# The first batch of three attentions scored in fp32, with the bf16 parts of the other batches made on GpSimd

## The reference, cut to what matters

```python
x = x + tanh(g_xattn[i]) * attention_i(layernorm(x), ctx)
x = x + tanh(g_ffn[i]) * ffn_i(layernorm(x))
```

```python
Q, K, V = heads(x @ Wq + bq), heads(ctx @ Wk + bk), heads(ctx @ Wv + bv)
scores  = Q @ K.T / sqrt(8) + adj          # then masked by mask or by padding
out     = softmax(scores) @ V @ Wo + bo
```

## Time and profile before

| what | value |
|---|---|
| time, median of 3 runs | 862.73 us (861.38 to 862.84) |
| the profiled execution's own time | 862.37 us |
| its span, first to last instruction | 860.4 us |
| mean granted TensorE clock | 0.898 of full speed |
| PE, VectorE, ScalarE, GpSimd busy | 702.3, 573.1, 488.9, 166.6 us |

### The profile page before, as it was taken

One profiled execution on the slowest core, in us unless ns is written; L12 is line 12 of the kernel. 1 busy time (PEld: TensorE's weight loads), 2 busy tenths in 40 slices (PEclk: granted clock), 3 DMA queues, 4 the chain that ended last, 5 costly groups with the idle time before them and its releaser, 6 DMA issues. The chain is left out here.

```text
span 860.4 us, 14382 instructions
## 1 busy us (share of the span) xinstructions
PE 702.3 (82%) x4728; PEld 396.0 (46%) x4728; DVE 573.1 (67%) x1765; ACT 488.9 (57%) x1323; POOL 166.6 (19%) x135
## 2 busy tenths in 40 slices
PE   4589994559997878999744899949999999869978
PEld 2266663336665323333222667635336666644322
DVE  3699995869996358667865999855316666436553
ACT  2288881259883568598812988812666556413201
POOL 8622000420000045536655000020000000000000
PEclk8689997769999768998885999979999999969999
DMA  8895004060000000000009200000000000000000
GB/s 310 169 319 177 2 7 69 23 126 2 2 2 2 0 1 0 1 0 1 1 0 180 41 2 2 2 26 0 1 0 1 1 2 2 1 1 1 0 1 24
DMA packets 22056, 32.26 MB, mean 38 GB/s; under 512 B 1760, under 2 KB 15712, under 8 KB 21216
## 3 DMA queue, kind: packets, MB, share of 16 engines
q1 hardware_dynamic: 21984, 31.36, 14.4%
HBM read 21.39 MB, written 9.96 MB: 36 GB/s over the span
## 5 line engine op out<-in xcount | busy, mean ns | idle before, releaser
L816 ACT ACTIVATE RING<-RING,NMX 128x256 f32<-128x256 f32 x384 | 190.7, 500 | 56.2 <-DVE NMX L1637 55.8
L1637 DVE CUSTOM_DVE_ANT_0 RING<-bank,ADJM 128x256 f32<-128x256 f32 x384 | 143.4, 413 | 23.5 <-DMA scratch<-RING 22.5
L1158 PE MATMUL bank<-W,RING 128*128 128x128 f32 x768 | 120.5, 282 | 15.6 <-ACT RING L828 13.9
L541 POOL TENSOR_TENSOR small<-small 128x8 f32<-128x8 f32 (+2 forms) x13 | 17.7, 1365 | 463.1 <-DVE small L1528 463.1
L1158 PEld LDWEIGHTS bank<-W,RING 128*128 128x128 f32 x768 | 91.7, 145 | 27.9 <-ACT RING L816 23.2
L1138 PE MATMUL bank<-ARENA 128*128 128x256 bf16 x384 | 77.8, 290 | 30.7 <-DMA ARENA<-scratch 25.7
L1649 DVE COPY RING<-bank 128x512 f32<-128x512 f32 x144 | 98.6, 686 | 1.2 <-PE bank L1158 0.8
L816 ACT ACTIVATION_READ_ACCUMULATOR RING<-RING,NMX 128x1 f32 x384 | 72.8, 190 | 0.0
L997 PE MATMUL bank<-XT,W 128*128 128x512 f32 (+2 forms) x118 | 62.2, 668 | 6.6 <-ACT XT L712 5.3
L728 ACT ACTIVATE RING<-bank,NMX 128x512 f32<-128x512 f32 x64 | 43.4, 683 | 41.8 <-PE bank L1062 21.2
L1280 PE MATMUL bank<-ARENA,W 64*128 64x512 f32 x180 | 62.3, 710 | 3.6 <-DVE ARENA L1830 2.3
(11 more groups left out here) (253 smaller groups left out, 1307.3 us busy)
## 6 DMA issues: line engine op xcount, KB each, us to landing
scratch<-ARENA SPq DMA_DIRECT2D x18, 256.0 KB, 3.2
ARENA<-scratch SPq DMA_DIRECT2D x6, 768.0 KB, 10.6
W<-in_weights SPq DMA_DIRECT2D x1, 2564.0 KB, 21.2
scratch<-RING SPq DMA_DIRECT2D x36, 64.0 KB, 3.0
ARENA<-scratch SPq DMA_DIRECT2D x12, 192.0 KB, 3.8
scratch<-RING SPq DMA_DIRECT2D x18, 128.0 KB, 2.9
ARENA<-scratch SPq DMA_DIRECT2D x6, 384.0 KB, 6.6
W<-in_weights SPq DMA_DIRECT2D x2, 1024.0 KB, 13.7
```

The lines of the kernel that those rows point to most:

```text
L816: nc.scalar.activation(P_OF(n)[:, q * S:(q + 1) * S], S_OF(n)[:, q, :], ACT.Exp, bias=NMX[:, 2 * t + q:2 * t + q + 1], scale=-1.0, accum_o ...
L1158: mm = nc.tensor.transpose(bk[:, o:o + P], P_OF(n)[:, i:i + P], ident)
L1637: nc.vector.tensor_tensor_reduce(out=S_OF(n)[:, q, :], in0=SBANK(n)[:, q * S:(q + 1) * S], in1=ADJM[:, b, q, :], scale=-1.0, scalar=BIG, o ...
```

## The change

In the first three attentions batch 0 (units 0 to 15) is scored from fp32 queries and keys, `Q32` and `K32`, without the way through parts and DRAM. PE makes them directly in head order: for each of four groups of heads it multiplies 32 columns of weights of each of 4 heads into the 4 column groups (`heads`), so that head j of a group lies on 8 rows from row 32 j on. ScalarE adds the bias, which must stand in the same order (`biases` and `BKQ`, new). Two units at a time are scored, from two groups of rows, and PE waits until VectorE has finished unit n - 2.

Queries and keys of batches 1 to 3 still go by way of bf16 parts and DRAM. Their parts are all made by GpSimd (`three_parts`), the queries from within the loop: the transposes for these tokens stand at t = 1 in PE's program, their query products at t = 3, the queries of head groups 2 and 3 of batch 0 at t = 5. In the first attention the values stand at t = 4, in the first and third the bias row (`out_row`) too; VectorE makes the masks of batches 1 to 3 of the first attention at t = 6. The clearings spare batch 0's part of the memory and, in the third attention, stand behind the layernorm but for a small piece ahead of it. The keys of the second and third attention are made after the first. SP loads `CT` first, then the first weights, then `X`; the masks come in two loads, and the second stretch of weights is loaded after the first attention's transfers.

```diff
-PIECES = [(0, S), (S, 2 * S), (2 * S, 4 * S)]
-QK_AT = [2, 9, 12]
+LATER = [(S, 2 * S), (2 * S, 4 * S)]
+REST = TOK - S
+HE_AT, HE_N = [0, 9, 15], [9, 6, 7]
+KEY_CUTS = [(S, S + 512), (S + 512, TOK)]
...
+        Q32 = ARENA[:, 0:8192].rearrange("p (h t) -> p h t", h=H16)
+        K32 = ARENA[:, 8192:12288].rearrange("p (j t) -> p j t", j=H16 // 2)
...
+            sp.dma_start(CT[:, :], ctxT_in).then_inc(s_ldc, 16)
+            sp.dma_start(W[:, 0:EDGES[1]], w_in[:, 0:EDGES[1]]).then_inc(s_ld[0], 16)
             sp.dma_start(X[:, :, :], x_in).then_inc(s_ldx, 16)
-            sp.dma_start(W[:, 0:EDGES[1]], w_in[:, 0:EDGES[1]]).then_inc(s_ld[0], 16)
-            sp.dma_start(CT[:, :], ctxT_in).then_inc(s_ldc, 16)
-            sp.dma_start(ADJ[:, :, :, :], adj_in).then_inc(s_ldm, 16)
-            sp.dma_start(MASK, mask_in).then_inc(s_ldm, 16)
-            sp.dma_start(PADW[:, :], pad_in).then_inc(s_ldm, 16)
-            sp.dma_start(W[:, EDGES[1]:EDGES[2]], w_in[:, EDGES[1]:EDGES[2]]).then_inc(s_ld[1], 16)
...
             def queries(a):
-                for k in range(len(PIECES) + 1):
-                    if k < len(PIECES):
-                        write(3 + a, QP, ((0, 3, 5), (1, 4), (2,)), slice(*PIECES[k]), s_qp,
-                              3 * (len(PIECES) * a + k), s_qw[k])
-                    if k >= 1:
-                        read(3 + a, lambda e: QS[64 * e:64 * e + 48, e::2, :], slice(*PIECES[k - 1]), s_qw[k - 1],
-                             96 * (a + 1), s_qs[k - 1])
+                for k, (t0, t1) in enumerate(LATER):
+                    write(3 + a, QP, ((0, 3, 5), (1, 4), (2,)), t0, t1, s_qp, 3 * (len(LATER) * a + k), s_qw[k])
+                    read(3 + a, lambda e: QS[64 * e:64 * e + 48, e::2, :], t0, t1, s_qw[k], 96 * (a + 1), s_qs[k])
             write_keys(0)
             sp.wait_ge(s_zero, 1)
             read_keys(0)
             queries(0)
-            for i in range(2, 5):
+            sp.dma_start(ADJ[:, 1:3, :, :], adj_in[:, 1:3, :, :]).then_inc(s_ldm3, 16)
+            for i in range(1, 5):
                 sp.dma_start(W[:, EDGES[i]:EDGES[i + 1]], w_in[:, EDGES[i]:EDGES[i + 1]]).then_inc(s_ld[i], 16)
             sp.dma_start(WINT[:, :, :], wint_in).then_inc(s_ldw, 16)
             write_keys(1)
-            write_keys(2)
             sp.wait_ge(s_s, UNITS)
             read_keys(1)
             queries(1)
+            write_keys(2)
             sp.wait_ge(s_zero, 2)
...
+            def clear_queries(h0, h1):
+                link(nc.gpsimd.memset(Q32[:, h0:h1, P:4 * P], 0.0))
+            def clear_keys():
+                link(nc.gpsimd.memset(K32[:, :, P:4 * P], 0.0))
+            def clear_pads():
+                nc.gpsimd.memset(V[:, :, D:VW], 0.0).then_inc(s_zero, 1)
+            def three_parts(src, parts, done, n, first=True, second=True):
+                if first:
+                    nc.gpsimd.tensor_copy(parts[:, 0, :], src).then_inc(done, 1)
+                    pool.wait_ge(done, n + 1)
+                    link(nc.gpsimd.tensor_tensor(src, src, parts[:, 0, :], ALU.subtract))
+                if second:
+                    nc.gpsimd.tensor_copy(parts[:, 1, :], src).then_inc(done, 1)
+                    pool.wait_ge(done, n + 2)
+                    nc.gpsimd.tensor_tensor(parts[:, 2, :], src, parts[:, 1, :], ALU.subtract).then_inc(done, 1)
+            def key_parts(a, first=True, second=True):
+                pool.wait_ge(s_ek, (6, 10, 12)[a])
+                pool.wait_ge(s_kw, 96 * a)
+                three_parts(KFS[a], KP, s_kp, 3 * a, first, second)
+            def query_parts(a):
+                for k, (t0, t1) in enumerate(LATER):
+                    pool.wait_ge(s_he, HE_AT[a] + 3 + k)
+                    pool.wait_ge(s_qw[k], 96 * a)
+                    cut = slice(t0 - S, t1 - S)
+                    three_parts(QF[:, cut], QP[:, :, cut], s_qp, 3 * (len(LATER) * a + k))
+            clear_queries(0, H16)
+            clear_keys()
+            clear_pads()
             pool.wait_ge(s_set, 1)
             roots()
+            key_parts(0)
+            query_parts(0)
             pool.wait_ge(s_set, 2)
-            masks(0)
-            for a in (1, 2):
-                for step in range(4):
-                    key_parts(a, step)
+            masks(0, 1, B)
+            masks(1, 0, 2)
             root()
+            key_parts(1, second=False)
             pool.wait_ge(s_am, 2)
             nc.gpsimd.partition_all_reduce(AMAXR, AMAX, P, bass.bass_isa.ReduceOp.max).then_inc(s_amr, 1)
+            key_parts(1, first=False)
             roots()
-            masks(1)
+            query_parts(1)
+            masks(1, 2, B)
+            key_parts(2)
             root()
             pool.wait_ge(s_ea, XT_AT[2])
+            pool.wait_ge(s_kp, 9)
             nc.gpsimd.memset(RH[32:33, :], 1.0).then_inc(s_pad, 1)
+            pool.wait_ge(s_pad, 1)
+            masks(2, 0, 2)
...
+            pool.wait_ge(s_xnext, 2 * NC)
+            clear_queries(10, H16)
             pool.wait_ge(s_int, 2 * NC)
-            clear_queries()
-            clear_rest()
             roots()
-            masks(2)
+            pool.wait_ge(s_xn, 5 * NT)
+            clear_keys()
+            clear_queries(0, 10)
+            clear_pads()
+            query_parts(2)
+            masks(2, 2, B)
...
+            def first_queries(a, g0, g1, ring, done):
+                for g in range(g0, g1):
+                    nc.scalar.activation(Q32[:, 2 * g:2 * g + 2, 0:P],
+                                         ring.take(act)[:, 0:S].rearrange("p (k c) -> p k c", k=2), ACT.Identity,
+                                         bias=BKQ[:, g, 3 + a:4 + a], scale=float(DH) ** -0.5).then_inc(done, 1)
...
+                        act.wait_ge(s_bkq, 3)
+                        first_keys(0, 0, NG)
                         keys(0)
...
+                    if a == 1:
+                        values(0, NC, ra, s_ea)
+                    empty_xt([(0, S)])
+                    first_queries(a, 0, 2, rk, s_ek)
+                    later_xt()
...
+                        if t == 3:
+                            later_queries(a)
+                        if t == 4 and a == 0:
+                            values(0, NC, rh, s_he)
+                        if t == 4 and a != 1:
+                            out_row(rh, s_he)
+                        if t == 5:
+                            first_queries(a, 2, NG, rh, s_he)
...
+            def biases():
+                at = COL["cols"][0] + CI["bk0"][0]
+                for h in range(H16):
+                    g, j = h // HG, h % HG
+                    mm = nc.tensor.matmul(bank[5][PAD * j:PAD * j + PAD, 6 * g:6 * g + 6],
+                                          w("ident", DH * h, DH * h + PAD), W[:, at:at + 6], start=True, stop=True)
+                mm.then_inc(s_bk, 1)
+            def heads(out, name, g, rhs):
+                for j in range(HG):
+                    f = DH * (HG * g + j)
+                    mm = nc.tensor.matmul(out[PAD * j:PAD * j + PAD, :], w(name, f, f + PAD), rhs, start=True,
+                                          stop=True)
+                return mm
+            def first_keys(a, g0, g1):
+                for g in range(g0, g1):
+                    heads(rk.fill(pe)[:, 0:S], f"wk{a}", g, CT[:, 0:S]).then_inc(s_fk, 1)
...
+                    if t < UNITS and b == 0 and t % 2 == 0:
+                        if j == 0 and g < 2:
+                            pe.wait_ge(s_ek, rk.n - 1 + g)
+                        elif j == 0:
+                            pe.wait_ge(s_he, HE_AT[a] + HE_N[a] - 3 + g)
+                        if n >= 2:
+                            pe.wait_ge(s_max, 2 * n - 2)
+                        for q in range(2):
+                            for i in range(2):
+                                r = slice(PAD * (j + i), PAD * (j + i) + DH)
+                                mm = nc.tensor.matmul(
+                                    SBANK(n + i)[:, q * S:(q + 1) * S].rearrange("p (k c) -> p k c", k=2),
+                                    Q32[r, 2 * g + q, 0:P], K32[r, 2 * g:2 * g + 2, 0:P], start=True, stop=True)
+                                if q == 1:
+                                    mm.then_inc(s_s, 1)
+                    if t == 1:
+                        for t0, t1 in LATER:
+                            turn(XN, t0 // P, t1 // P, rh, s_hf)
+                    if t == 3:
+                        later_queries(a)
+                    if t == 4 and a == 0:
+                        values(0, 0, NC, rh, s_hf)
+                    if t == 4 and a != 1:
+                        out_row(a, rh, s_hf)
+                    if t == 5:
+                        first_queries(a, 2, NG, rh, s_hf)
+                    if t < UNITS and b > 0:
+                        pe.wait_ge(s_max, 2 * n - 4)
                         bk = SBANK(n)
+                        if t == 16:
```

(34 more changed lines are left out.)

253 lines of the change are left out of this document (123 added, 130 removed).

## The result

The changed kernel took 839.65 us (median of 4 runs, 828.79 to 849.29) beside 862.06 us (4 runs, 860.23 to 862.84): ratio 0.970 [0.961, 0.980]. An unchanged copy, measured later, took 837.83 us (6 runs, 828.6 to 842.58), ratio 0.969 [0.965, 0.973]. So it is 22 to 24 us faster where 33.2 were forecast: the sign and the range held, the size did not. The kernel before varies by 5 to 7 us from run to run, this one by 20, and over its ten runs the time goes with the span's mean granted clock (849.3 us at 0.903, 838.2 at 0.922, 828.6 at 0.938; correlation -0.997). Three of the ten (849.29, 842.58 and 842.3) are over 1.5% above the kernel's fastest and are left out of the ratios; the first of them is the profiled one, so the copy's profiled execution stands beside it where sizes are compared.

A forecast was written before the change was run, and what follows sets the result against it. It took waits of 15 us or more ahead of the first three attention loops as removable, VectorE and PE pacing the loops. Gains 9.9, 11.4 and 15.9, less 4 between, made 33.2 us: 829.5 us, range 813 to 847.

The forecast's parts named there:

- First maxima: Start of the first three attentions: first row maximum comes 23.9, 15.4 - 4 and 23.9 us earlier.
- The price of a pair: Batch 0's loop on PE: two units' fp32 scores take 1.2 us, or 0.85 without a drain.
- row groups of 8 rows don't overlap: Rival on batch 0's score pairs: each costs 1.7 + 0.34 us, in all 20 us lost, 850 us; chance 0.12.
- Shape, moved work and masks: Loops of the first three attentions: shape switches, work moved into the loop and masks cost 12, 4 and 6.5 us.
- Clock: Loop starts: half clock in the first ten microseconds costs 2, none and 1.5 us; bounds 0 and 8 each.
- a clock of 0.50 through the first ten units: Sign of being wrong, in the attention loops: granted clock at half level through the first ten units.
- Between: First feed-forward: GpSimd's key parts hold VectorE's XN and scale instructions, 4 us lost; bounds 0 and 4.8.
- Batch 1 late: Rival at t = 16, first and third attention: PE waits some 5 us each, 840 us; chance 0.07.
- GpSimd stops VectorE in the loop: Rival in the three loops: VectorE waits for GpSimd's 54 us of work, 21 us lost, 883 us; chance 0.04.

The follow-up runs named there:

- e5: Changed kernel with score products over 32 rows (24 of them zero) and the masks of batches 1 to 3 made in three pieces: 827.07 us.
- e12: e11 with one more unused 512-column product at t = 7 and one at t = 8 of the first attention: 823.65 us.
- e4: Changed kernel with batch 0 scored in plain bf16, leaving out part of the precision: 819.86 us.
- e7: Changed kernel with unused PE products, three at t = 1 of the first attention, two ahead of the third's transposes: 833.65 us.
- e8: Changed kernel with the first attention's values and bias row at t = 1, the third's bias row ahead of the transposes: 831.3 us.
- e1: The changed kernel itself, an unchanged copy measured again: 837.83 us.
- e3: Changed kernel with the first attention's masks of batches 1 to 3 made in three pieces at t = 2, 3 and 4: 832.02 us.
- e2: Changed kernel with batch 0's fp32 score products over 32 rows, 24 of them zero, instead of 8: 832.75 us.
- e9: Changed kernel with the edits of e5 and e8 together: 828.38 us.
- e10: e9 with GpSimd making the second attention's key parts only after VectorE's last XN: 826.69 us.
- e11: e10 with two unused 512-column PE products ahead of the third attention's transposes: 819.16 us.
- e6: Changed kernel with the second attention's key parts made in one piece, behind the layernorm's roots: 843.46 us.

## Why the prediction was right in sign and range, and too low

*First maxima.* Right: 19.84 (20 forecast), and in the changed kernel the gains of 24.0, 10.6 and 23.0 us stand against 23.9, 11.4 and 23.9.

*The price of a pair.* Right: 1.06 us from start to start against 1.2. The rival that row groups of 8 rows don't overlap is out, by the rows and not by the time, which lay between it and the forecast.

*Shape, moved work and masks: 12, 4 and 6.5 us.* Too high by themselves. The fastest stretches seen of fp32 scores, with the granted clock at 1.00 throughout, are 25.9 us (e5), 22.7 (e5) and 22.6 (e12), which is 7.1, 3.9 and 4.3 over the kernel before, 15.3 in all. These have 32-row products, and masks or values in other places (the forecast of 12 had the masks in one piece, and PE's 3.17 us of waiting with them), so the 7 us by which the term was too high are an estimate.

*Clock: 2 us in the first, none in the second, 1.5 in the third, bounds 0 and 8 each.* This step failed: the term of the sum was far too small. Against those same stretches the copy loses 8.2, 3.0 and 6.9 us and the changed kernel's slower execution 14.2, 3.0 and 11.3: 18 and 28 us where 3.5 stood, and past my bound of 8 in one attention and in two. That this is the clock's size shows in the mean granted clock of units 0 to 15: 0.80, 0.87 and 0.79 in the copy, 0.63, 0.87 and 0.67 in the other. By these they spent 13.6, 6.7 and 12.4 us at the 1.2 GHz level, and 29.7, 6.7 and 22.4; half of that, an estimate of the loss where PE's work sets the pace, is 16 and 29 us. I had priced the first ten microseconds of each loop. But the clock could fall again in the loop, after the 3.17 us in which the masks held PE, and it stayed at half through units in which PE never paused. The two errors, +7 and -15 to -25, make up most of the miss: 6 us in the copy's profiled execution, 20 in the changed kernel's, 10 in the median. That the median stayed in the range is in part luck, since the two errors have opposite signs; the execution of 849.29 lay outside it. The run-to-run spread goes with the clocks listed with the times. The prediction had named a clock of 0.50 through the first ten units as a sign of being wrong, and the third attention comes near it: the windows from 440 to 455 stand at 0.50, and unit 8 starts at 462.8.

The prediction also overlooked that the half clock had no visible cost before. The kernel before started its loops at half clock as well, with a mean granted clock of 0.62, 0.67 and 0.70 over units 0 to 7, and took 8.9, 8.8 and 8.4 us for them, against 9.9 for the next eight at 1.00, which hold more output work. So the change did not bring the half clock at the starts of the loops; it brought PE so much work in these units that a half clock had a price.

What makes the clock stay down is shown only in part. It fell in or right behind PE waits in the loop (the changed kernel, e4, e7, e8). With 8-row products it also fell with PE busy (e1, e3). With 32 rows every fall inside a loop stood at a PE wait: 3.17 us (e2), 0.76 and 0.74 (e9, e10, e11), 2.96 (e12), and 2.1 to 2.5 at the late read (e10, e11, e12). In e5, without such waits behind the first units, there was none, though PE had waited 0.88 us at 19.1. Whether a wait ahead of the loop decides was not shown: with the same 1.05 us wait the clock fell in e10 and stayed in e9. Which property of the narrower product matters was not tried.

*Between: 4 us lost.* Right: 4.4. But half of my picture was missing. I had VectorE wait for GpSimd; GpSimd also waited 6.84 us, by the times for VectorE. The Trainium skill, SBUF — State Buffer, section SBUF: two separate sides, says that whichever of the two starts first keeps the shared pair of ports for its whole instruction and the other is blocked; e6 agrees, with 5.66 us against 1.63 for the same six instructions. The page speaks of one instruction; GpSimd's 6.84 us reach over a whole chain of VectorE's, which no run here explains. Moving the GpSimd work along the path gave 2.0 us from unit 63 to unit 0 (e6, in its trace against the copy's), and moving it past VectorE's last such instruction 6.2 (e10 against e9).

*Batch 1 late.* Wrong for the changed kernel: no wait at unit 16, and units 16 to 63 as before. It comes true in e10, where the read of the keys runs ahead of the query writes. I had looked for the lateness in GpSimd's and SP's order, and it came from transfers beside one another.

*GpSimd stops VectorE in the loop.* Wrong: L1789 has a mean of 415 ns over all three loops, against 413. The page's group:

```profile
L1789 DVE CUSTOM_DVE_ANT_0 RING<-bank,ADJM 128x256 f32<-128x256 f32 x384 | 144.3, 415 | 27.5 <-PE bank L1248 22.3
```

Its 27.5 us of idle time are mostly waits for fp32 scores, PE's price again.

## What to carry to other kernels

Shortening a wait ahead of a PE-bound loop by giving PE more to do in the loop pays the wait's length less the added work at the clock that PE is then granted: price both levels for the whole stretch, not for its first microseconds. Look at what makes PE wait inside the loop (3 us of masks here), and at how few rows the products use. GpSimd work beside VectorE instructions that it stretches is free only where neither is on the chain, and what is moved behind the last of them takes its transfers along, into those of the next stage.

## What was not expected of the hardware

Products of 8 rows and of 32 rows, same columns, same length at full clock, left different clocks behind them: 0.76 and 0.66 against 1.00 with PE busy in all. With 8 rows the same program's time varied by 2.5% from run to run (828.6 to 849.3). And the same code met the clock differently in the same place: units 0 to 7 of the third attention took 11.01 us in e9 and 14.27 in e10.
